# Splitting the gathered rows of a segment sum into two float32r parts on the chip

## The chip, the cores and the metric
The kernel runs on one core of one Trainium2 chip. The metric is the time of one execution on the device in microseconds (us). Below, PE is TensorE's matmul stream, PEld its weight loads, DVE is VectorE, ACT is ScalarE, POOL is GpSimd and SP is SyncE.

## The reference
Two graph layers over 3125 nodes with 256 features and 100,000 edges. The second layer, in which the change lies, is cut here to what matters:

```
proj = jnp.einsum('ni,rio->rno', feat, Wb)          # 16 relations, 3125 nodes, 256 features
m    = proj[etypes, dst] + backward_bias            # one gathered row of 256 floats per edge
m    = m / degree(src)[src]
m_backward = segment_sum(m, src, num_segments=3125)  # summed into the node that the edge leaves
out = x + 2*(feat @ loop_weight) + self_bias + m_forward + m_backward
```

## The kernel before
The work is in stages, one after the other. Layer one goes over the edges in 196 supertiles of 512 (512 = 4 groups of 128, `J = 4`). Then PE projects all nodes for each of the relations, the forward rows are gathered and summed while PE makes the backward projections, and last come the backward rows. VectorE has sorted the edges by source on the way.

The last stage, called the backward stage below, is the one that the change touches. It runs over 196 supertiles (`ST`) with four engines:

- GpSimd gathers the rows (`gather_rows`, L429): four indirect DMAs for a supertile, each of 128 rows of 1 KB, with the row numbers read from `row_dst` in SBUF. They go into a ring of buffers `raw2` with `RS = 12` places in SBUF (inside the tile `hr`). Before the first of four it waits until PE has read the place for the last time (`s_agg[2]`). All of this is unrolled code, so GpSimd has nothing between the gathers but that wait.
- VectorE compares the source numbers of the 512 edges with the 256 nodes of a window of two blocks (`compare2`, recorded at L1013) and so writes a one-hot matrix of 128 x 1024 floats into a ring of six (`HS = 6`, in the tile `fa`). One of its inputs, `iota_p`, lies in PSUM.
- PE multiplies (`products2`, L731): for each half of the window four matmuls of 128x258 in float32, 8 in all, into one of three pairs of PSUM banks. Columns 256 and 257 of a row are ones, so that the sum counts the edges too.
- VectorE adds the pair of sums to `acc` (`add2`, L1070). Where the sources of a supertile reach beyond the two blocks, a further one-hot, four further matmuls and a further addition follow (L1013, L731 with `pc`, L1078).

VectorE's code is a loop over six supertiles, PE's one over twelve. At the top of each pass VectorE loads the packed windows of ten supertiles from SBUF into registers (`windows_of`, L281), which takes no engine time but holds back what follows. The order of VectorE's work is written out by hand in `backward`: for supertile s it first compares for s + 4, then adds the sums of s.

Ahead of the backward stage lies a short passage in which VectorE and ScalarE finish the forward means and clear `acc` (L1296, L1349, L592, L595). The gathers of the backward stage already run in it. After the stage `backward_mean` scales the sums (L1291) and SP stores the output.

float32r is the type of the operands of PE's single-pass matmuls in this kernel. Layer one already works so: ScalarE casts a tile to float32r (the high part, L520), VectorE subtracts that from the tile (the low part, L1026), and PE multiplies both parts.

Of the kernel before, what the change touches and what calls it, by code (L numbers as in the profile page):

```python
# [41 lines left out]
QS = 24  # L42
RS = 12
HS = 6
# [4 lines left out]
assert ST % GS == 0 and COLS % RG == 0 and ST % RG == 0 and SI == S1 * (NQ // 2) + 2 == 2 * (S2 + QS)  # L49
assert (ST - GS) % RS == 0 and (ST - GS) % (2 * RF) == 0 and 2 * QS % RF == 0  # L50


def gnn_program(nc, x, dst_l, src_l, typ_l, ea_t, W1, b1, W2, b2, Wg, bg, gamma, beta,
# [9 lines left out]
    with ctx:  # L63
# [6 lines left out]
        def sem(name):  # L70
            return ctx.enter_context(nc.semaphore(name))
# [80 lines left out]
        slot_iota, slot_base = srt[:, 0:P].bitcast(I32), srt[:, P:P + NB].bitcast(I32)  # L152
        raw2 = hr[:, 0:RS * J * AW].bitcast(F32).rearrange("p (a j f) -> p a j f", a=RS, j=J)
        onehot2 = [fa[:, c:c + 2 * SE].rearrange("p (j n) -> p j n", j=J) for c in (8192, 9216, 4224, 5248, 2064, 3096)]
        further_onehot = fa[:, 6272:6272 + SE].rearrange("p (j n) -> p j n", j=J)
        PARTS = ((1, 0), (0, 1), (0, 0))
# [69 lines left out]
        s_xadd = [sem(f"s_xadd{k}") for k in range(3)]  # L226
        s_ones = sem("s_ones")
        s_xagg = [sem(f"s_xagg{k}") for k in range(3)]
        s_self = sem("s_self")
# [147 lines left out]
        def _(pool):  # L377
# [67 lines left out]
            for s in range(ST):  # L445
                if s >= RS:
                    pool.wait_ge(s_agg[2], s - RS + 2)
                gather_rows(raw2[:, s % RS, :, :], proj[1][:, :], row_dst, s, s_gath[2][s % RS])


        @block.scalar
        def _(act):
# [135 lines left out]
            for b in range(NB + 2):  # L588
# [4 lines left out]
                if b >= 2:  # L593
                    act.wait_ge(s_scaled, b - 1)
                    nc.scalar.copy(acc[:, b - 2, :], iota[:, 0:1].to_broadcast([P, AW])).then_inc(s_zero[1], 1)  # L595

        @block.tensor
        def _(pe):
# [126 lines left out]
            def sum_backward(s, n, rnd, w):  # L725

                lo, hi, wx = w

                def products2(out, keys):
                    for j in range(J):  # L730
                        last = nc.tensor.matmul(out[:, 0:AW], keys[:, j, :], raw2[:, n, j, :], start=(j == 0), stop=(j == J - 1))  # L731
                    return last

                pe.wait_ge(s_oh[2], s + 1)
                pe.wait_ge(s_gath[2][n], 16 * J * (rnd + 1))
                if past(s, 3):
                    pe.wait_ge(s_add[2], s - 2)
                for c in range(2):
                    last = products2(pair_sums[n % 3][:, c, :], onehot2[n % HS][:, :, c * P:(c + 1) * P])
                last.then_inc(s_agg[2], 1)  # L740
                with pe.If(hi > lo + 1):
                    with pe.Fori(lo + 2, hi + 1) as b:
                        pe.wait_ge(s_xadd[2], wx + b)
                        pe.wait_ge(s_xoh[2], wx + b)
                        products2(further_sums, further_onehot).then_inc(s_xagg[2], 1)
# [94 lines left out]
        def _(dve):  # L840
# [509 lines left out]
            dve.wait_ge(s_mean, NB)  # L1350
            nc.vector.memset(raw2[:, :, :, H:AW], 1.0).then_inc(s_ones, 1)
            dve.wait_ge(s_zero[1], NB)

            def backward(s0, n0, w, ahead):
                for m in range(len(w)):
                    if m + 4 < len(w):
                        compare2(s0 + m + 4, (n0 + m + 4) % HS, w[m + 4])
# [3 lines left out]
            for n, w2 in enumerate(windows_of(dve, 1, 2, 2)):  # L1361
                compare2(n + 2, n + 2, w2)
            backward(0, 0, windows_of(dve, 1, 0, 2 * GS), GS)
            with dve.Fori(0, (ST - GS) // HS - 1) as i:
# [49 lines left out]
```

## Time and profile before

| what | value |
|---|---|
| time, median of 3 runs | 3745.22 us (3745.19 to 3745.71) |
| time of the profiled execution | 3743.66 us |
| its span in the profile | 3741.9 us |
| busy PE, DVE, ACT, POOL | 86%, 66%, 27%, 67% of the span |
| DMA | 569.99 MB, mean 152 GB/s |
| granted TensorE clock, mean | 0.975 of full speed |

The span is that of one profiled execution; its own time is 1.8 us longer than the span, and the median of the other runs is 1.6 us above that time. Busy shares are means over stages with different limits; the backward stage begins at about 2737 us, when GpSimd starts its gathers, and ends at about 3725 us.

### The profile page before, as it was taken

The page shows a single profiled execution, that of the slowest core. Times are in us where ns is not written, and L with a number is a line of the kernel's source. Part 1 is how long each engine was busy: PE and PEld are TensorE (multiplying, and loading weights), DVE is VectorE, ACT ScalarE, POOL GpSimd, SP SyncE. Part 2 cuts the span into 40 slices and gives each one's busy share as a digit, 9 for nine tenths or more (in the row PEclk, how much of TensorE's full clock was granted, in tenths as well). Part 3 has the DMA queues.
Part 4 walks back from the last instruction along what each step waited for, and adds up shares of the span by engine and source line. Part 5 has one row for each costly group of instructions (what it writes and reads, how often), then busy time and mean ns, then how long its engine had stood idle before and what let it go on. Part 6 is the DMA issues. An engine that isn't in the chain of part 4 may idle for free.

```text
span 3741.9 us, 72813 instructions
## 1 busy us (share of the span) xinstructions
PE 3212.6 (86%) x21136; PEld 2761.7 (74%) x21137; DVE 2457.5 (66%) x3369; ACT 1001.5 (27%) x1563; POOL 2492.5 (67%) x3139
## 2 busy tenths in 40 slices
PE   5999999999999996999877788878867778777775
PEld 4999999999999995787665566656656666665654
DVE  6899999999999998887666663223254344444433
ACT  3555555555555554443111111111120000000000
POOL 1777777777777770001777777777777777777775
PEclk8999999999999998999999999999989999999999
DMA  4666666666566652665555557555543333333333
GB/s 165 178 176 177 173 176 172 176 168 177 171 174 171 171 171 74 201 207 187 165 166 164 162 167 175 166 156 165 165 116 105 105 105 105 105 105 105 105 105 114
DMA packets 322755, 569.99 MB, mean 152 GB/s; under 512 B 73896, under 2 KB 218392, under 8 KB 322584
## 3 DMA queue, kind: packets, MB, share of 16 engines
q0 software_dynamic: 137984, 411.19, 39.1%
q1 hardware_dynamic: 182732, 154.33, 13.0%
q10 hardware_dynamic: 1868, 2.52, 0.2%
q8 instruction: 67, 1.10, 0.1%
q14 instruction: 104, 0.85, 0.1%
HBM read 452.43 MB, written 115.41 MB: 152 GB/s over the span
## 4 chain that ended last, share of the span: by engine, by line
PE 45%; POOL 25%; issue 13%; DVE 11%; DMA 1%; DVEq 1%; ACT 1%; POOLq 0%; ACTq 0%
POOL hr L429 16%; PE pc L679 14%; PE pa L689 10%; PE pu L669 5%; PE pg L653 4%; DVE tops L1229 4%; POOL fa L429 4%; DVE key L1232 4%; PE pu L661 3%; POOL ws L429 2%; PE pu L731 1%; POOL rows_b L429 1%; PE pu L786 1%; PE pc L641 1%; PE pa L731 1%
## 5 line engine op out<-in xcount | busy, mean ns | idle before, releaser
L410 POOL DMA_INDIRECT fa<-ptab,slot x784 | 774.9, 988 | 323.9 <-issue 254.6
L429 POOL DMA_INDIRECT hr<-proj,row_dst x784 | 741.6, 946 | 238.7 <-issue 237.2
L429 POOL DMA_INDIRECT fa<-proj,row_src x400 | 378.8, 947 | 466.3 <-DMA proj<-fa 343.5
L679 PE MATMUL pc<-ws,hr 128*128 128x256 f32 x4704 | 603.4, 284 | 0.0
L679 PEld LDWEIGHTS pc<-ws,hr 128*128 128x128 f32 x4704 | 570.3, 189 | 0.5 <-issue 0.5
L689 PE MATMUL pa<-fa,onehot 128*128 128x256 f32 x904 | 241.3, 417 | 125.3 <-issue 57.4
L731 PE MATMUL pu<-hr,fa 128*128 128x258 f32 x1056 | 248.0, 387 | 78.6 <-issue 43.0
L689 PEld LDWEIGHTS pa<-fa,onehot 128*128 128x128 f32 x904 | 178.9, 205 | 183.8 <-issue 157.4
L1013 DVE SCALAR_TENSOR_TENSOR fa<-pc,base,src_f 128x1024 f32<-128x1024 f32 (+1 forms) x210 | 261.8, 1248 | 74.8 <-issue 63.6
L1046 DVE TENSOR_TENSOR acc<-acc,pa 128x256 f32 x196 | 82.1, 419 | 342.6 <-PE pa L689 341.2
L731 PE MATMUL pg<-hr,fa 128*128 128x258 f32 x1040 | 241.5, 384 | 63.7 <-issue 49.3
L520 ACT CAST hr<-fa 128x1024 fp32r<-128x1024 f32 x196 | 205.9, 1051 | 331.1 <-DVE fa L1020 331.1
L731 PE MATMUL pa<-hr,fa 128*128 128x258 f32 x1040 | 241.2, 384 | 61.2 <-issue 50.4
L731 PEld LDWEIGHTS pu<-hr,fa 128*128 128x128 f32 x1056 | 197.8, 191 | 126.7 <-issue 56.7
L509 ACT ACTIVATE hr<-pu 128x512 fp32r<-128x512 f32 x392 | 213.2, 597 | 252.9 <-PE pu L669 252.9
L1020 DVE TENSOR_TENSOR fa<-fa,pc 128x1024 f32<-128x1024 f32 x196 | 239.3, 1221 | 60.5 <-PE pc L679 59.3
L731 PEld LDWEIGHTS pg<-hr,fa 128*128 128x128 f32 x1040 | 192.9, 189 | 110.1 <-issue 64.8
L731 PEld LDWEIGHTS pa<-hr,fa 128*128 128x128 f32 x1040 | 193.0, 189 | 106.9 <-issue 66.1
L1026 DVE TENSOR_TENSOR hr<-fa,hr 128x1024 fp32r<-128x1024 f32 x196 | 241.2, 1231 | 24.1 <-ACT hr L520 8.7
L689 PE MATMUL pa<-hr 128*128 128x258 f32 (+1 forms) x1760 | 248.2, 284 | 5.7 <-issue 3.6
L786 PE MATMUL pu<-hr 128*128 128x512 f32 x960 | 246.0, 399 | 1.4 <-DVE hr L1172 0.7
L997 DVE SCALAR_TENSOR_TENSOR hr<-pu,hr 128x1024 fp32r<-128x1024 f32 x196 | 238.1, 1215 | 3.6 <-ACT hr L509 3.5
(167 smaller groups left out, 5653.2 us busy)
## 6 DMA issues: line engine op xcount, KB each, us to landing
proj<-fa SPq DMA_DIRECT2D x400, 256.0 KB, 2.4
fa<-in_ea_t SPq DMA_DIRECT2D x196, 128.0 KB
fa<-ptab,slot POOLq DMA_INDIRECT x784
hr<-proj,row_dst POOLq DMA_INDIRECT x784, 2.7
fa<-in_Wrel SPq DMA_DIRECT2D x32, 256.0 KB, 3.7
ptab<-fa SPq DMA_DIRECT2D x25, 256.0 KB, 2.0
fa<-proj,row_src POOLq DMA_INDIRECT x400, 3.0
ws<-proj,row_src POOLq DMA_INDIRECT x192
```

The lines of the kernel that those rows point to most:

```text
L410: pool.indirect_dma_start(pbuf[:, n % 2, j, :], None, ptab[:, :], bass.IndirectOffsetOnAxis(ap=slot[:, n, j:j + 1], axis=0)).then_inc(s_ga ...
L429: pool.indirect_dma_start(buffer[:, j, 0:H], None, table, bass.IndirectOffsetOnAxis(ap=rows[:, J * s + j:J * s + j + 1], axis=0)).then_inc ...
L509: last = nc.scalar.activation(uT[:, par, 0, h, :, :].rearrange("p k e -> p (k e)"), pu[:, h, :], ACT.Relu)
L520: nc.scalar.copy(msg[:, par, 0, :, :], gate[:, par, :, :]).then_inc(s_mhi, 1)
L679: last = nc.tensor.matmul(pc[:, j, :], uT[:, par, a, j // 2, kk, j % 2 * P:(j % 2 + 1) * P], w2s[:, c, kk, :], start=False, stop=(j == jj ...
L689: last = nc.tensor.matmul(pa[:, bank, 0:width], keys[:, at, j, :], rows[:, j, :], start=(n == 0), stop=(n == len(todo) - 1))
L731: last = nc.tensor.matmul(out[:, 0:AW], keys[:, j, :], raw2[:, n, j, :], start=(j == 0), stop=(j == J - 1))
L786: last = nc.tensor.matmul(pslots[n], hT[:, a, kk, b * P:(b + 1) * P], wsp[:, u, c, kk, :], start=(not d and m == 0 and kk == 0), stop=(m = ...
L997: nc.vector.scalar_tensor_tensor(out=uT[:, par, 1, :, :, :].rearrange("p h k e -> p h (k e)"), in0=pu[:, :, :], scalar=0.0, in1=uT[:, par, ...
L1013: return nc.vector.scalar_tensor_tensor(out=out, in0=numbers.unsqueeze(1).to_broadcast([P, J, width]), scalar=base[:, bass.ds(b, 1)], in1= ...
L1020: nc.vector.tensor_tensor(gate[:, par, :, :], gate[:, par, :, :], pc[:, :, :], ALU.mult).then_inc(s_msg, 1)
L1026: nc.vector.tensor_tensor(msg[:, par, 1, :, :], gate[:, par, :, :], msg[:, par, 0, :, :], ALU.subtract).then_inc(s_mlo, 1)
```

## The change
- Each gathered supertile is split on the chip. ScalarE casts it to float32r into `high2` (`rows_high`), VectorE subtracts that from the raw rows into `low2` (`rows_low`), both rings of three places (`RP2 = 3`) in float32r. The ones of the count stand in `high2` alone.
- `products2` makes 16 float32r matmuls for a supertile instead of 8 in float32: for each half of the window four of 128x258 with the high part and four of 128x256 with the low part.
- The ring of raw rows has six places instead of twelve (three in `hr`, three in `fa`), and GpSimd takes a place again once `rows_low` has read it (`s_rowlo`), no longer after PE. PE waits for `s_rowlo` instead of the gathers' semaphores.
- The one-hots become float32r and move from `fa` to `hr`. PE's loop covers six supertiles instead of twelve.
- In `backward`, VectorE does `rows_low` of supertile s + 1 first, then `compare2` of s + 4, then `add2` of s.

```diff
-RS = 12
+RS = 6
+RP2 = 3
...
-        raw2 = hr[:, 0:RS * J * AW].bitcast(F32).rearrange("p (a j f) -> p a j f", a=RS, j=J)
-        onehot2 = [fa[:, c:c + 2 * SE].rearrange("p (j n) -> p j n", j=J) for c in (8192, 9216, 4224, 5248, 2064, 3096)]
...
+        raw2 = [t.rearrange("p (j f) -> p j f", j=J) for t in
+                [hr[:, c:c + J * H].bitcast(F32) for c in (12824, 13848, 14872)] + [fa[:, c:c + J * H] for c in (4224, 5248, 8192)]]
+        high2 = hr[:, 0:RP2 * J * AW].rearrange("p (a j f) -> p a j f", a=RP2, j=J)
+        low2 = hr[:, 3096:3096 + RP2 * J * H].rearrange("p (a j f) -> p a j f", a=RP2, j=J)
+        onehot2 = [hr[:, c:c + 2 * SE].rearrange("p (j n) -> p j n", j=J) for c in range(6168, 6168 + 2 * SE * HS, 2 * SE)]
...
                 if s >= RS:
-                    pool.wait_ge(s_agg[2], s - RS + 2)
-                gather_rows(raw2[:, s % RS, :, :], proj[1][:, :], row_dst, s, s_gath[2][s % RS])
+                    pool.wait_ge(s_rowlo, s - RS + 1)
+                gather_rows(raw2[s % RS], proj[1][:, :], row_dst, s, s_gath[2][s % RS])
...
+            def rows_high(s, n, rnd):
+
+                act.wait_ge(s_gath[2][n], 16 * J * (rnd + 1))
+                if past(s, RP2):
+                    act.wait_ge(s_agg[2], s - RP2 + 2)
+                nc.scalar.copy(high2[:, n % RP2, :, 0:H], raw2[n]).then_inc(s_rowhi, 1)
...
                 def products2(out, keys):
-                    for j in range(J):
-                        last = nc.tensor.matmul(out[:, 0:AW], keys[:, j, :], raw2[:, n, j, :], start=(j == 0), stop=(j == J - 1))
+                    todo = [(j, part) for part in (high2, low2) for j in range(J)]
+                    for t, (j, part) in enumerate(todo):
+                        rows = part[:, n % RP2, j, :]
+                        last = nc.tensor.matmul(out[:, 0:rows.shape[1]], keys[:, j, :], rows, start=(t == 0), stop=(t == len(todo) - 1))
                     return last
 
                 pe.wait_ge(s_oh[2], s + 1)
-                pe.wait_ge(s_gath[2][n], 16 * J * (rnd + 1))
+                pe.wait_ge(s_rowlo, s + 1)
...
-            nc.vector.memset(raw2[:, :, :, H:AW], 1.0).then_inc(s_ones, 1)
+            nc.vector.memset(high2[:, :, :, H:AW].bitcast(F32), 1.0).then_inc(s_ones, 1)
             dve.wait_ge(s_zero[1], NB)
+
+            def rows_low(s, n):
+
+                dve.wait_ge(s_rowhi, s + 1)
+                nc.vector.tensor_tensor(low2[:, n % RP2, :, :], raw2[n], high2[:, n % RP2, :, 0:H],
+                                        ALU.subtract).then_inc(s_rowlo, 1)
 
             def backward(s0, n0, w, ahead):
                 for m in range(len(w)):
+                    if m < len(w) - max(ahead, 1):
+                        rows_low(s0 + m + 1, (n0 + m + 1) % RS)
                     if m + 4 < len(w):
                         compare2(s0 + m + 4, (n0 + m + 4) % HS, w[m + 4])
...
             for n, w2 in enumerate(windows_of(dve, 1, 2, 2)):
                 compare2(n + 2, n + 2, w2)
+            rows_low(0, 0)
```

How VectorE's instructions stand at the top of its loop over six supertiles, before. The first row is the load of the windows into registers, L1013 the comparison, L1070 the addition; the names of semaphores end in 2 for the backward stage.

```order
L281 TENSOR_LOAD win
L1058 REGISTER_ALU
L1013 REGISTER_ALU [waits s_agg2]
L1013 ISA
L1013 SCALAR_TENSOR_TENSOR fa<-pc,base,src_f 128x1024
L1065 REGISTER_ALU x3
L1065 ISA
L1068 REGISTER_ALU [waits s_add2,s_xadd2]
L1070 ISA [waits s_agg2]
L1070 TENSOR_TENSOR acc<-acc,pg 128x516
```

The same place after the change (line numbers of the changed kernel: L287 the load, L1378 the subtraction of `rows_low`, L1034 the comparison, L1091 the addition).

```order
L287 TENSOR_LOAD win
L1377 REGISTER_ALU
L1378 TENSOR_TENSOR hr<-fa,hr 128x1024 [waits s_rowhi]
L1079 REGISTER_ALU
L1034 REGISTER_ALU [waits s_agg2]
L1034 ISA
L1034 SCALAR_TENSOR_TENSOR hr<-pc,base,src_f 128x1024
L1086 REGISTER_ALU x3
L1086 ISA
L1089 REGISTER_ALU [waits s_add2,s_xadd2]
L1091 ISA [waits s_agg2]
L1091 TENSOR_TENSOR acc<-acc,pg 128x516
```

One subtraction with both inputs in SBUF now stands ahead of the comparison in every supertile, and at the top of the loop it stands behind the load.

ScalarE had no instruction in this stage before. Its loop after the change is this (L608 the cast; the waits on `s_gath2_n` are for the four gathers of a supertile):

```order
L607 REGISTER_ALU [waits s_gath2_0]
L608 CAST hr<-hr 128x4x256 [waits s_agg2]
L607 REGISTER_ALU [waits s_gath2_1]
L608 CAST hr<-hr 128x4x256 [waits s_agg2]
L607 REGISTER_ALU [waits s_gath2_2]
L608 CAST hr<-hr 128x4x256 [waits s_agg2]
```

The wait for the gathers stands on a register instruction ahead of the cast, as it does in layer one before at the top of ScalarE's loop (L519 ahead of the cast L520):

```order
L519 REGISTER_ALU [waits s_msg]
L520 CAST hr<-fa 128x4x256 [waits s_add0]
```

## Rows read from the trace of the kernel before

**Rows 1.** Windows view: busy us and (count) of each engine, granted clock, DMA share, GB/s.

```profile
3200.00:3400.00 200.00, 156.44 (x681) 126.09 (x681) 84.25 (x91) 0.00 (x0) 151.27 (x161) 1.00 0.36 105
```

**Rows 2.** Source view of L429, 2737 to 3742 us: ns min/median/max, first and last start.

```profile
L429 POOL DMA_INDIRECT hr<-proj,row_dst x784: 942/946/1248, 2737.7 to 3716.9; - x196
...
  issue: 237.2, 779
...
DMA to landing us min/median/max: 2.6/2.7/4.2
```

**Rows 3.** Waits view, 2800 to 3700 us: us in total, times, longest us.

```profile
DVE acc L1070 <- PE pu L731: 162.5, 61, 3.2
...
DVE fa L1013 <- issue: 61.3, 28, 2.9
```

**Rows 4.** Timeline of the end: start us, us, engine, line, idle before and its releaser.

```profile
3716.94 0.95 POOL L429 DMA_INDIRECT hr<-proj,row_dst  x1 [0.30 <-issue]
...
3719.72 3.35 PEld L731 LDWEIGHTS pu<-hr,fa 128*128 128x128 f32 x16 [1.59 <-issue]
3719.75 3.73 PE L731 MATMUL pu<-hr,fa 128*128 128x258 f32 x16 [1.22 <-issue]
3723.72 0.69 DVE L1070 TENSOR_TENSOR acc<-acc,pu 128x516 f32 x1 [4.25 <-PE pu L731]
```

**Rows 5.** Timeline of the forward gathers, where VectorE splits weights (L1172).

```profile
2152.98 1.23 DVE L1172 TENSOR_TENSOR hr<-fa,hr 128x1024 fp32r<-128x1024 f32 x1
2153.23 1.80 POOL L429 DMA_INDIRECT ws<-proj,row_src  x1 [0.30 <-issue]
...
2522.20 0.95 POOL L429 DMA_INDIRECT fa<-proj,row_src  x1 [0.30 <-issue]
2522.76 1.22 DVE L1172 TENSOR_TENSOR hr<-fa,hr 128x1024 fp32r<-128x1024 f32 x1
2523.45 1.35 POOL L429 DMA_INDIRECT fa<-proj,row_src  x1 [0.30 <-issue]
```

**Rows 6.** Timeline of layer one: a gather and a subtraction that start nearly together.

```profile
1358.42 0.97 POOL L410 DMA_INDIRECT fa<-ptab,slot  x1 [0.15 <-issue]
1358.47 1.23 DVE L1026 TENSOR_TENSOR hr<-fa,hr 128x1024 fp32r<-128x1024 f32 x1
```

**Rows 7.** Timeline of layer one: cast, subtraction and eight float32r matmuls.

```profile
1053.20 1.11 PE L689 MATMUL pa<-hr 128*128 128x258 f32 x8
1054.66 1.05 ACT L520 CAST hr<-fa 128x1024 fp32r<-128x1024 f32 x1 [1.27 <-DVE fa L1020]
1055.74 1.25 DVE L1026 TENSOR_TENSOR hr<-fa,hr 128x1024 fp32r<-128x1024 f32 x1
...
1204.08 1.22 DVE L1020 TENSOR_TENSOR fa<-fa,pc 128x1024 f32<-128x1024 f32 x1
1205.41 1.05 ACT L520 CAST hr<-fa 128x1024 fp32r<-128x1024 f32 x1 [1.33 <-DVE fa L1020]
```

**Rows 8.** Timeline where the backward stage gets under way.

```profile
2763.20 6.50 PE L731 MATMUL pu<-hr,fa 128*128 128x258 f32 x16 [19.39 <-DVE hr L1351]
2763.70 3.67 DVE L1013 SCALAR_TENSOR_TENSOR fa<-pc,base,src_f 128x1024 f32<-128x1024 f32 x3 [0.55 <-issue]
...
2768.05 0.96 POOL L429 DMA_INDIRECT hr<-proj,row_dst  x1 [0.30 <-issue]
```

**Rows 9.** Source view of L1078, and timeline of one further block and one loop top.

```profile
L1078 DVE TENSOR_TENSOR acc<-acc,pc x14: 423/424/426, 2952.4 to 3487.5; 128x258 f32 x14
...
3097.29 1.28 DVE L1013 SCALAR_TENSOR_TENSOR fa<-pc,base,src_f 128x1024 f32<-128x1024 f32 x1 [2.90 <-issue]
...
3108.60 0.69 DVE L1070 TENSOR_TENSOR acc<-acc,pu 128x516 f32 x1 [3.06 <-PE pu L731]
3109.30 0.75 DVE L1013 SCALAR_TENSOR_TENSOR fa<-pc,base,src_f 128x512 f32<-128x512 f32 x1
3110.20 1.98 PE L731 MATMUL pc<-hr,fa 128*128 128x258 f32 x8 [1.75 <-DVE fa L1013]
3112.39 0.43 DVE L1078 TENSOR_TENSOR acc<-acc,pc 128x258 f32 x1 [2.34 <-PE pc L731]
```

More of the change, by code:

```diff
@@ L49 @@
 assert ST % GS == 0 and COLS % RG == 0 and ST % RG == 0 and SI == S1 * (NQ // 2) + 2 == 2 * (S2 + QS)
-assert (ST - GS) % RS == 0 and (ST - GS) % (2 * RF) == 0 and 2 * QS % RF == 0
+assert HS == RS and RS % RP2 == 0 and (ST - GS) % RS == 0 and (ST - GS) % (2 * RF) == 0 and 2 * QS % RF == 0
 def gnn_program(nc, x, dst_l, src_l, typ_l, ea_t, W1, b1, W2, b2, Wg, bg, gamma, beta,
@@ L152, in gnn_program @@
         slot_iota, slot_base = srt[:, 0:P].bitcast(I32), srt[:, P:P + NB].bitcast(I32)
-        raw2 = hr[:, 0:RS * J * AW].bitcast(F32).rearrange("p (a j f) -> p a j f", a=RS, j=J)
-        onehot2 = [fa[:, c:c + 2 * SE].rearrange("p (j n) -> p j n", j=J) for c in (8192, 9216, 4224, 5248, 2064, 3096)]
-        further_onehot = fa[:, 6272:6272 + SE].rearrange("p (j n) -> p j n", j=J)
+        raw2 = [t.rearrange("p (j f) -> p j f", j=J) for t in
[3 more added lines that the diff above has]
+        onehot2 = [hr[:, c:c + 2 * SE].rearrange("p (j n) -> p j n", j=J) for c in range(6168, 6168 + 2 * SE * HS, 2 * SE)]
+        further_onehot = hr[:, 12312:12312 + SE].rearrange("p (j n) -> p j n", j=J)
         PARTS = ((1, 0), (0, 1), (0, 0))
@@ L227, in gnn_program @@
         s_ones = sem("s_ones")
+        s_rowhi = sem("s_rowhi")
+        s_rowlo = sem("s_rowlo")
         s_xagg = [sem(f"s_xagg{k}") for k in range(3)]
@@ L595, in _ @@
                     nc.scalar.copy(acc[:, b - 2, :], iota[:, 0:1].to_broadcast([P, AW])).then_inc(s_zero[1], 1)
+            def rows_high(s, n, rnd):
[3 more added lines that the diff above has]
+                nc.scalar.copy(high2[:, n % RP2, :, 0:H], raw2[n]).then_inc(s_rowhi, 1)
+            for n in range(GS):
+                rows_high(n, n, 0)
+            with act.Fori(0, (ST - GS) // RS) as i:
+                for m in range(RS):
+                    rows_high(RS * i + GS + m, (GS + m) % RS, i + (GS + m) // RS)
         @block.tensor
```

## The prediction
> **What bounds the kernel now.** The windows view of the backward stage comes first [rows 1]. In 200 us PE is busy for 156.4, VectorE for 84.3 and GpSimd for 151.3, so no engine is full and the shares alone don't decide. The source view of the gathers decides [rows 2]. 784 gathers start between 2737.7 and 3716.9 us, one each (3716.9 - 2737.7) / 783 = 1.2506 us, of which 0.946 are the instruction and 0.30 its issue; 779 of 784 idle times ahead of them end by nothing but issue. GpSimd never waits for PE's hand-back. It makes a supertile of four gathers in 5.00 us, and the other two engines live inside that: VectorE waits for PE for up to 3.2 us at the additions [rows 3], and PE's 16 records of a supertile take 3.73 us and begin 2.78 us after the supertile's last gather has started, that is on its landing [rows 4]. So the stage lasts 196 x 5.00 us whatever PE does below 5.00, and faster matmuls are worth something only behind the last gather.
>
> **The change part by part.**
>
> *PE.* Eight float32r matmuls of 258 and 256 columns take 1.11 us at full clock [rows 7], 16 some 2.1 us against 3.73. Inside the stage this is worth nothing, since the gathers cover it; were that cover gone, it would be 196 x 1.6 = 314 us. At half the clock, which PE has after it stood idle for 19 us (the first supertile takes 6.50 instead of 3.73 us [rows 8]), 16 would take 4.2 us, which is still below 5.00.
>
> *The end.* The last gather starts at 3716.94 and PE's load at 3719.72 [rows 4]. ScalarE can begin its cast a little later than PE its load: where the wait stands on a register instruction, as in the new loop, the cast L520 starts 0.11 us after its releaser (1204.08 + 1.22 to 1205.41), elsewhere 0.04 [rows 7]. That is 2.78 + 0.07 = 2.85 us after the gather's start. Cast 1.05, 0.03 to VectorE (1054.66 + 1.05 to 1055.74), subtraction 1.22 [rows 5, 7]: the low part is there at 5.15, and PE ends 0.06 + 2.1 later, at 7.3 us behind the gather instead of 6.54. The end costs +0.8 us, with half the clock +2.9. I take +1.
>
> *Rings.* A place is handed back about 3.75 + 5.15 = 8.9 us after the supertile's first gather, and is wanted again after 6 x 5.00 = 30. Only the start is close: supertile 6 wants its place at 2768.05 [rows 8]. VectorE is through with the two comparisons that stand ahead of `rows_low(0)` at about 2766.2 (two of the three in 3.67 us), so the first place is free at 2767.4. No stall, with 0.6 us to spare.
>
> *What the subtraction does to the gathers.* This is the term that decides. `rows_low` has both inputs in SBUF. The forward stage has such a subtraction too, L1172, and gathers beside it [rows 5]. L1172 runs from 2152.98 to 2154.21; a gather that starts at 2153.23 takes 1.80 us instead of 0.95: 0.85 more, and 2154.21 - 2153.23 - 0.85 = 0.13. L1172 runs from 2522.76 to 2523.98; the gather at 2523.45 takes 1.35, 0.40 more, and again 0.53 - 0.40 = 0.13. The gather at 2522.20, under way when L1172 began, took 0.95. So a gather that starts while such a subtraction runs needs something 0.13 us after its start which it gets only when the subtraction ends, and all later gathers move by the same time. A gather that starts ahead of the subtraction is safe, even by 0.05 us: it takes its usual 0.97 [rows 6].
>
> The Trainium skill ("SBUF — State Buffer", Who interferes with whom) says that a VectorE instruction with two SBUF inputs contends with a GpSimd instruction that reads SBUF, and that whichever came first holds the port for its whole length; the trace agrees, as the rows show. The same section also says that a probe saw `tensor_tensor` not stall DMA and infers that making descriptors needs another port; by that sentence the stage would keep its 1.25 us a gather and the sum would be +1 us. The measured rows decide against it here, and it stays as a rival.
>
> Now the phase. Count from the start of a supertile's last gather. The next gathers start at 1.25, 2.50, 3.75, 5.00. The subtraction begins at 2.85 + 1.05 + 0.03 = 3.93 and ends at 5.15. A gather is held if it starts behind the subtraction and its start + 0.13 lies before the subtraction's end. The one at 3.75 started first, by 0.18; the one at 5.00 wants its port at 5.13, 0.02 before the end. So the usual supertile costs 0.02 us, and with the spread of the landings (2.6 at least, 2.7 in the median [rows 2]) about 0.03: 166 x 0.03 = 5 us. It matters that the phase renews itself: landing, cast and subtraction all follow the last gather, so a shift of the gathers shifts them too.
>
> *Loop tops.* VectorE's cycle is subtraction 1.22, comparison 1.28, addition 0.69. Where they follow directly each starts some 0.08 before the last has ended (three comparisons in 3.67 us [rows 8]), so the cycle is 3.0 us and the next subtraction is due only after 5.00. At the top of its loop the load of the windows stands in between. The idle time from an addition to the next comparison there is 2.90 us at the long ones [rows 9]; 28 such times sum to 61.3 [rows 3], so some are short (about 1.5) and about 16 of 32 long. `rows_low` has two register instructions less ahead of it than the comparison, for which I take off 0.2: 3.0 + 2.7 = 5.7, late by 0.7. It then ends at 5.85 and the gather at 5.00 is held for 5.85 - 5.13 = 0.7. 16 x 0.7 = 11 us. The short ones come in time.
>
> *Further blocks.* 14 supertiles have one [rows 9]. Addition's start to that of the further one is 3.79 us (3108.60 to 3112.39), of which 1.98 are matmuls that now take 1.11: 2.9, plus 0.43. VectorE is free at 2.35 + 2.9 + 0.43 = 5.7 after its subtraction began, late by 0.65, and the gather at 5.00 is held for about 0.65. 14 x 0.65 = 9 us.
>
> *Start.* Until VectorE has caught up with the gathers, some six to eight subtractions fall without a fixed phase: 0.5 us each, 4 us.
>
> The sum: 5 + 11 + 9 + 4 + 1 = +30 us. Against the profiled execution's own time, 3743.7 + 30 = 3773.7; the median of the runs shown is 1.6 us above it, so 3775.
>
> **The rivals.**
> 1. *The phase lies later.* If the landing, the cast or its wait takes 0.1 to 0.3 us more, each usual supertile costs that on top: 166 x 0.1 = 17 us to 166 x 0.3 = 50 us, 3790 to 3825. For it: the margin is 0.02 us and nothing of the order gather, ScalarE, VectorE has been seen together.
> 2. *The phase slips ahead.* If the subtraction starts 0.2 us or more earlier, at 3.71 say, the gather at 3.75 is held for 3.71 + 1.22 - 3.88 = 1.05 us in nearly every supertile: up to 196 x 1.05 = +205 us, at half of them about +100. 3850 to 3950. Against it: 0.2 us is more than the spread of most landings.
> 3. *The gathers are not held* (the end on the other side): the held gathers of the forward stage have another cause, and what is left is the end, +1 us, 3746; with PE's clock at half in the end +3, 3748. It decides if in the usual supertiles and at the loop tops the gathers stay at 0.946 us. For it: the 784 gathers of this stage ran at 946 ns while VectorE worked 42% of the time; against it, those operations have an input in PSUM and are another kind.
> 4. *The stage is PE's after all* and the float32r products shorten it: each 0.1 us a supertile would give 20 us. Against it stand 779 idle times that end by issue. Little is left for it.
>
> **How the numbers follow.** Forecast (+15 to +45 us): 0.60. Rival 1: 0.15. Rival 2: 0.09. Rival 3: 0.10, nearly all within 0.2% (7.5 us, what a measurement of this kernel can tell from no change). Between 3752.7 and 3760: 0.04. Rival 4: 0.02. The range 3756 to 3828 takes in the forecast, rival 1 and part of what lies between. Faster 0.02, same 0.11, slower 0.87.
>
> **What the changed profile would show.** The gathers: a median near 0.95 to 1.00 us, a mean near 0.98 (30 us over 784), some 40 of them over 1.25, and the last one starting near 3746. Those long ones begin inside a subtraction and end its end + 0.82. PE's busy share near 42% in the stage. ScalarE with 196 casts of 1.05 us. VectorE's subtraction begins 3.9 us behind the last gather. I would be wrong if the held gathers show up in every supertile (rival 2), if there are none (rival 3), or if GpSimd's idle time names the wait for `rows_low` for more than a microsecond, which would mean that the ring of six binds.

## The result and the profile after

The changed kernel takes 3766.08 us, the median of 5 runs (3760.5 to 3767.08), and the kernel before, run beside it, 3745.22 (5 runs, 3743.63 to 3748.19). The ratio is 1.005, 95% interval 1.0038 to 1.0061: slower, by about 21 us.

The windows view of the changed kernel over the same stretch as [rows 1], in the same columns:

```profile
3200.00:3400.00 200.00, 118.78 (x669) 111.00 (x669) 124.83 (x129) 41.29 (x40) 151.87 (x158) 0.79 0.36 103
```

PE's busy time fell from 156.4 to 118.8 us, VectorE's rose from 84.3 to 124.8, ScalarE came in with 40 casts, and GpSimd, which sets the pace, has done 158 gathers where it had done 161.

The source view of the gathers (L435 now), 2737 to 3770 us, to be read against [rows 2]. `raw2` now lies partly in `fa`, so there are two groups, with min/median/max in ns and the first and last start:

```profile
L435 POOL DMA_INDIRECT hr<-proj,row_dst x396: 942/946/1889, 2741.3 to 3731.9; - x198
L435 POOL DMA_INDIRECT fa<-proj,row_dst x388: 942/946/1965, 2756.7 to 3736.9; - x194
...
  issue: 239.6, 787
```

The median is as before, but the longest took 1.97 us instead of 1.25, and still no idle time of GpSimd ends by a wait for another engine. The groups view of the same stretch has the sums (busy us, mean ns of one, idle us and its releaser):

```profile
L435 POOL DMA_INDIRECT hr<-proj,row_dst x396 | 385.8, 974 | 120.5 <-issue 120.5
L435 POOL DMA_INDIRECT fa<-proj,row_dst x388 | 372.1, 959 | 118.2 <-issue 118.2
```

385.8 + 372.1 = 757.9 us, where 784 x 0.946 = 741.7 were to be had: 16.2 us more. From first to last start it is 3736.86 - 2741.34 = 995.5 us instead of 979.2 [rows 2], 16.3 more. All of the stage's loss is in the durations of its gathers.

The spans differ by 3764.4 - 3741.9 = 22.5 us, and they divide so:

| part | us |
|---|---|
| ahead of the first gather (2737.7 to 2741.3) | 3.6 |
| first to last gather | 16.3 |
| last gather's start to the end (24.9 to 27.5) | 2.6 |

The first part can't be shown to be the change's: in the nine profiled executions of this study the first backward gather starts anywhere between 2737.2 and 2741.3, and both ends are kernels that contain the change (e4 and the changed kernel).

What one held gather looks like, in the timeline of the changed kernel at the start of the stage (start us, us, engine, line, idle before and its releaser):

```profile
2787.16 0.94 POOL L435 DMA_INDIRECT hr<-proj,row_dst  x1 [0.30 <-issue]
2787.75 1.22 DVE L1378 TENSOR_TENSOR hr<-hr 128x1024 fp32r<-128x1024 f32 x1
2788.41 1.38 POOL L435 DMA_INDIRECT hr<-proj,row_dst  x1 [0.30 <-issue]
```

The gather under way when the subtraction begins is untouched. The next starts inside it and ends at 2789.79, which is the subtraction's end, 2788.97, and 0.82: the same sum as for L1172 [rows 5].

And a usual supertile, one whose subtraction is 0.05 us later than the median, in the timeline of the same kernel near the end of the stage:

```profile
3724.30 0.95 POOL L435 DMA_INDIRECT hr<-proj,row_dst  x1 [0.30 <-issue]
3724.69 1.05 ACT L608 CAST hr<-hr 128x1024 fp32r<-128x1024 f32 x1 [4.06 <-DMA hr<-proj,row_dst]
...
3725.55 0.94 POOL L435 DMA_INDIRECT hr<-proj,row_dst  x1 [0.30 <-issue]
3725.77 1.22 DVE L1378 TENSOR_TENSOR hr<-hr 128x1024 fp32r<-128x1024 f32 x1 [2.08 <-ACT hr L608]
...
3726.80 1.01 POOL L435 DMA_INDIRECT hr<-proj,row_dst  x1 [0.30 <-issue]
```

The subtraction begins 0.22 us behind one gather and ends at 3726.99; the next gather starts at 3726.80 and wants its port at 3726.93, so it is held for 0.06. In the trace the subtraction begins 3.92 us after the start of the supertile's last gather in the median of the 156 usual ones (three in four by 3.96, nine in ten by 3.99) and ends at 5.15; 3.93 and 5.15 were predicted.

There is one exception to the rule that a gather behind the subtraction's start is held:

```profile
2970.17 1.29 DVE L1378 TENSOR_TENSOR hr<-hr 128x1024 fp32r<-128x1024 f32 x1 [0.26 <-ACT hr L608]
2970.20 0.95 POOL L435 DMA_INDIRECT hr<-proj,row_dst  x1 [0.30 <-issue]
```

The gather starts 0.034 us behind and takes its usual time, and it is the subtraction that takes 1.29 us instead of 1.22. In the changed kernel, e3, e4 and e5 this happens to nine gathers, all of which start within 0.043 us. From 0.048 us on every one is held: in the changed kernel, e2, e3 and e5 that is 601 gathers, and the rule gives the hold of each to within 0.02 us.

### The profile page after: what moved, and what is told of

It reads as the page before. It is cut to its first block, busy times and chain, and to the rows that moved or that the text cites. A ratio compares the mean times of both kernels' runs of the same rounds, so it can differ in the third digit from the quotient of the medians.

```text
span 3764.4 us, 73607 instructions
## 1 busy us (share of the span) xinstructions
PE 3058.4 (81%) x21136; PEld 2713.5 (72%) x21137; DVE 2664.0 (71%) x3565; ACT 1207.0 (32%) x1759; POOL 2511.6 (67%) x3139
## 4 chain that ended last, share of the span: by engine, by line
PE 40%; POOL 31%; issue 13%; DVE 10%; DMA 1%; DVEq 1%; ACT 1%; POOLq 0%; ACTq 0%
POOL fa L435 15%; PE pc L698 14%; POOL hr L435 10%; PE pa L708 9%; PE pu L688 5%; PE pg L672 4%; DVE tops L1250 4%; DVE key L1253 4%; PE pu L680 3%; POOL ws L435 3%; POOL rows_b L435 1%; POOL rows_a L435 1%; PE pc L660 1%; PE pu L807 1%; PE pg L807 1%
## 5 line engine op out<-in xcount | busy, mean ns | idle before, releaser
L435 POOL DMA_INDIRECT fa<-proj,row_src x400 | 380.6, 952 | 467.2 <-DMA proj<-fa 344.1
L435 POOL DMA_INDIRECT hr<-proj,row_dst x396 | 385.8, 974 | 120.5 <-issue 120.5
L435 POOL DMA_INDIRECT fa<-proj,row_dst x388 | 372.1, 959 | 118.2 <-issue 118.2
L752 PE MATMUL pg<-hr 128*128 128x258 f32 (+1 forms) x1040 | 191.0, 355 | 122.0 <-issue 62.6
L752 PE MATMUL pu<-hr 128*128 128x258 f32 (+1 forms) x1056 | 183.7, 342 | 125.8 <-issue 102.1
L752 PE MATMUL pa<-hr 128*128 128x258 f32 (+1 forms) x1040 | 189.7, 353 | 111.5 <-issue 57.5
L752 PEld LDWEIGHTS pg<-hr 128*128 128x128 f32 x1040 | 177.3, 258 | 134.4 <-issue 134.4
L752 PEld LDWEIGHTS pu<-hr 128*128 128x128 f32 x1056 | 171.3, 246 | 138.2 <-issue 138.1
L752 PEld LDWEIGHTS pa<-hr 128*128 128x128 f32 x1040 | 176.6, 257 | 124.8 <-issue 124.8
L1034 DVE SCALAR_TENSOR_TENSOR hr<-pc,base,src_f 128x1024 fp32r<-128x1024 f32 (+1 forms) x210 | 260.9, 1243 | 1.4 <-DVE win L920 0.8
L708 PE MATMUL pa<-hr 128*128 128x258 f32 (+1 forms) x1760 | 248.9, 284 | 5.3 <-issue 3.2
```

Source lines behind the costliest of these rows:

```text
L435: pool.indirect_dma_start(buffer[:, j, 0:H], None, table, bass.IndirectOffsetOnAxis(ap=rows[:, J * s + j:J * s + j + 1], axis=0)).then_inc ...
L708: last = nc.tensor.matmul(pa[:, bank, 0:width], keys[:, at, j, :], rows[:, j, :], start=(n == 0), stop=(n == len(todo) - 1))
L752: last = nc.tensor.matmul(out[:, 0:rows.shape[1]], keys[:, j, :], rows, start=(t == 0), stop=(t == len(todo) - 1))
L1034: return nc.vector.scalar_tensor_tensor(out=out, in0=numbers.unsqueeze(1).to_broadcast([P, J, width]), scalar=base[:, bass.ds(b, 1)], in1= ...
```

## The experiments

The phase of a subtraction is the time from the start of its supertile's last gather to its own start. Theory A is the prediction's: a subtraction with both inputs in SBUF holds a gather that starts behind it, until the subtraction ends. The rivals are that the loss comes from VectorE's or ScalarE's added work as such, from the smaller ring, from PE's slower clock, or that the hold belongs to some other property of the subtraction. A hold is the time that a gather takes over its usual 0.946 us.

**e1_one_input**: all of the change stays, with its order, waits and bytes, but the subtraction's first input is in PSUM. The subtraction itself is left out: `low2` receives the raw rows. The operation is of another kind too, `scalar_tensor_tensor`; e7 keeps the kind.

```diff
-                nc.vector.tensor_tensor(low2[:, n % RP2, :, :], raw2[n], high2[:, n % RP2, :, 0:H],
-                                        ALU.subtract).then_inc(s_rowlo, 1)
+                nc.vector.scalar_tensor_tensor(out=low2[:, n % RP2, :, :], in0=fbias_p.unsqueeze(1).to_broadcast([P, J, H]), scalar=0.0,
+                                               in1=raw2[n], op0=ALU.mult, op1=ALU.add).then_inc(s_rowlo, 1)
```

> The changed kernel, with rows_low as a VectorE operation of the same size that has one input in SBUF and one in PSUM (0 times the bias in PSUM plus the raw rows). It leaves out the subtraction: the low part is the whole row. Theory A (the subtraction with two SBUF inputs holds the gathers): no gather of the backward stage over 1.1 us, the sum of what the gathers take over 0.946 us falls from 16 us to under 1, the last one starts 980 us after the first as in the kernel before, and the time is 16 us under the changed kernel's: 3750 us, 2 to 7 us over the kernel before (the end, and whatever lies ahead of the stage). Theory B (some other part of the split, such as the six places, ScalarE's reads or more work on VectorE, slows the gathers): long gathers stay, 3766 us.

Measured: 3746.21 us (11 runs), ratio to the kernel before 1.0002 (0.9993 to 1.0011). Timeline of this kernel behind a further block, where VectorE is late and its instructions lie anywhere:

```profile
3087.91 1.23 DVE L1378 SCALAR_TENSOR_TENSOR hr<-pc,hr 128x1024 fp32r<-128x1024 f32 x1 [0.19 <-ACT hr L608]
3087.98 0.95 POOL L435 DMA_INDIRECT fa<-proj,row_dst  x1 [0.30 <-issue]
```

The gather starts 0.07 us behind an instruction of 1.23 us, the worst place there is, and takes 0.95. The longest gather is the second, with 1.25 us, as it is in the kernel before (1248 ns in [rows 2]), and no other is over 0.97, though 118 gathers begin inside such an instruction; their durations over 0.946 sum to -0.1 us, and first to last start is 979.2 us as before. So this edit is worth 995.5 - 979.2 = 16.3 us of the gathers. The medians differ by 3766.1 - 3746.2 = 19.9 us; 2.5 of that is the start of the stage (2738.9 instead of 2741.3 in the traces). The rest of the change costs the gathers nothing. Its end is there, 27.5 us from the last gather's start instead of 24.9, but 2.6 us can't be told from the spread of the runs here (3743.9 to 3748.2), and the median came 0.7 us over the kernel before where 2 to 7 were expected.

**e2_before_plus_sub**: the other direction. The kernel before gets only the suspect, a subtraction with both inputs in SBUF whose result nobody reads, and a ring of six handed back by the additions to make room. It waits for the gathers directly, so it comes earlier in the phase.

```diff
-RS = 12
+RS = 6
...
-                    pool.wait_ge(s_agg[2], s - RS + 2)
+                    pool.wait_ge(s_add[2], s - RS + 2)
...
+            def read_rows(s, n, rnd):
+
+                dve.wait_ge(s_gath[2][n], 16 * J * (rnd + 1))
+                at = 12800 + n % 3 * J * H
+                nc.vector.tensor_tensor(hr[:, at:at + J * H].rearrange("p (j f) -> p j f", j=J), raw2[:, n, :, 0:H], raw2[:, n, :, 0:H],
+                                        ALU.subtract)
...
+                    if m < len(w) - max(ahead, 1):
+                        read_rows(s0 + m + 1, (n0 + m + 1) % RS, r0 + (n0 + m + 1) // RS)
...
```

> The kernel before with six raw places and an added VectorE subtraction of a gathered supertile from itself into unused SBUF, as soon as the gathers have landed; PE still multiplies the raw rows in float32. Theory A with the phase rule (a gather that starts behind the subtraction's start wants its port 0.13 us after its own start and waits to the subtraction's end): it starts 2.8 us behind the last gather, ends at 4.03, and the gather at 3.75 is held to 4.03 - 3.88 = 0.15 us in every supertile: 196 x 0.15 = 29 us, with 5 to 9 us for further blocks and the start and 5 for the six places, 3745 + 42 = 3787 us, most gathers third of their supertile at about 1.10 us. If holds are there but fall at random: 0.5 us each, 3745 + 100. Theory B: 3750 us, what six places cost alone.

Measured: 3787.81 us (4 runs), ratio 1.0114 (1.0099 to 1.013). One supertile in its timeline:

```profile
3300.23 1.23 DVE L1358 TENSOR_TENSOR hr<-hr 128x1024 fp32r<-128x1024 f32 x1 [2.08 <-DMA hr<-proj,row_dst]
...
3301.23 1.04 POOL L429 DMA_INDIRECT hr<-proj,row_dst  x1 [0.30 <-issue]
```

The gather at 3301.23 is held by 3301.46 - 3301.23 - 0.13 = 0.10 us, as measured. The holds sum to 38.2 us, 25.5 of them at the third gather of a supertile; the rest of the 42 us is one wait of GpSimd for the smaller ring, some 5 us (e6). The suspect alone brings a loss of the same kind, and a supertile pays what its phase says.

**e3_later_cast**: the changed kernel with the cast in four pieces, which makes nothing but its end later.

```diff
-                nc.scalar.copy(high2[:, n % RP2, :, 0:H], raw2[n]).then_inc(s_rowhi, 1)
+                for j in range(J):
+                    last = nc.scalar.copy(high2[:, n % RP2, j, 0:H], raw2[n][:, j, :])
+                last.then_inc(s_rowhi, 1)
```

> The changed kernel with ScalarE's cast in four pieces of 128x256, so that the subtraction begins later; the same values. Four casts of 0.40 us that overlap a little take 1.3 to 1.6 us instead of 1.05: the subtraction begins 4.2 to 4.4 us behind the last gather instead of 3.92. Theory A with the phase rule: each usual supertile costs the shift, 0.25 to 0.5 us at the fourth gather: 166 x 0.25 to 0.5 = +42 to +83 us over the changed kernel, 3808 to 3849 us. If the phase doesn't matter: +1 us at the end, 3767 us.

Measured: 3804.84 us (4 runs), ratio 1.0161 (1.0146 to 1.0177). Its timeline:

```profile
3299.18 1.32 ACT L609 CAST hr<-fa 128x256 fp32r<-128x256 f32 x4 [3.97 <-DMA fa<-proj,row_dst]
...
3300.54 1.22 DVE L1380 TENSOR_TENSOR hr<-fa,hr 128x1024 fp32r<-128x1024 f32 x1 [2.27 <-ACT hr L609]
3301.35 1.23 POOL L435 DMA_INDIRECT fa<-proj,row_dst  x1 [0.30 <-issue]
```

The four casts take 1.32 us instead of 1.05, so the subtraction comes 0.27 later, and the gather that starts 5.00 us behind the supertile's last one is held by 0.27 us in the median of all supertiles: 47.6 us there and 54.8 in all. That is 0.27 us of ScalarE's time turned into 39 us of the whole. The time is 3 us under the expected 3808 to 3849. It is rival 1 of the prediction, brought about on purpose, near its price (166 x 0.27 = 45 us).

**e4_split_halves**: cast and subtraction in two halves each, so that the low part is ready earlier.

```diff
-                nc.scalar.copy(high2[:, n % RP2, :, 0:H], raw2[n]).then_inc(s_rowhi, 1)
+                for h in (0, 2):
+                    nc.scalar.copy(high2[:, n % RP2, h:h + 2, 0:H], raw2[n][:, h:h + 2, :]).then_inc(s_rowhi, 1)
...
-                dve.wait_ge(s_rowhi, s + 1)
-                nc.vector.tensor_tensor(low2[:, n % RP2, :, :], raw2[n], high2[:, n % RP2, :, 0:H],
-                                        ALU.subtract).then_inc(s_rowlo, 1)
+                for h in (0, 2):
+                    dve.wait_ge(s_rowhi, 2 * s + 1 + h // 2)
+                    last = nc.vector.tensor_tensor(low2[:, n % RP2, h:h + 2, :], raw2[n][:, h:h + 2, :], high2[:, n % RP2, h:h + 2, 0:H],
+                                                   ALU.subtract)
+                last.then_inc(s_rowlo, 1)
```

> The changed kernel with cast and subtraction each in two halves of 128x512, so that the first subtraction begins before the gather at 3.75 us behind the last one; the same values. The first half of the cast takes 0.6 us from 2.83, the first subtraction runs from about 3.45 to 4.13. Phase rule: the gather at 3.75 starts behind it, wants its port at 3.88 and is held to 4.13, 0.25 us in each usual supertile: 160 x 0.25 = +40 us over what the changed kernel has in its usual supertiles (2 us), some 3803 us, nearly all at the third gather of a supertile. If the second subtraction, which follows at about 4.1, takes the port before the waiting gather gets it, the hold goes to 4.75 or so: 0.85 us each, +135 us, 3900. If only the length of a subtraction mattered, shorter ones would hold less: 3766 us or less.

Measured: 3805.09 us (4 runs), ratio 1.0161 (1.0145 to 1.0177). Its timeline, the two halves in one row:

```profile
3301.90 1.29 DVE L1380 TENSOR_TENSOR hr<-fa,hr 128x512 fp32r<-128x512 f32 x2 [2.26 <-ACT hr L609]
3302.12 1.29 POOL L435 DMA_INDIRECT fa<-proj,row_dst  x1 [0.30 <-issue]
```

The supertile's last gather started at 3298.37 (two gathers ahead of the one shown, 3299.62 and 3300.88, belong to the next), so the low part is there 4.82 us behind it instead of 5.14. The price is a hold at the third gather of nearly every supertile (164 of 196), 49.1 us there and 58.6 in all, since the subtraction now begins ahead of that gather. The gather shown lost 1.29 - 0.95 = 0.34 us, which ends its hold at 3302.12 + 0.13 + 0.34 = 3302.59, in the middle of the pair and not at its end. So a waiting gather gets through between two subtractions that follow one another directly, and a pair costs no more than its first half.

**e5_pe_float32**: is PE's speed worth anything now? The changed kernel with PE's eight float32 products as before, on the high part and the one-hots. The low product is left out.

```diff
-                    todo = [(j, part) for part in (high2, low2) for j in range(J)]
-                    for t, (j, part) in enumerate(todo):
-                        rows = part[:, n % RP2, j, :]
-                        last = nc.tensor.matmul(out[:, 0:rows.shape[1]], keys[:, j, :], rows, start=(t == 0), stop=(t == len(todo) - 1))
+                    for j in range(J):
+                        last = nc.tensor.matmul(out[:, 0:AW], keys[:, j, :].bitcast(F32), high2[:, n % RP2, j, :].bitcast(F32),
+                                                start=(j == 0), stop=(j == J - 1))
```

> The changed kernel with PE's products as before: 8 float32 matmuls of 128x258 on the high part alone, in place of 16 in float32r. It leaves out the product with the low part, while cast and subtraction go on. If PE's speed is worth nothing in the stage: the same 16 us of holds but for 2 or 3 us at the 14 further blocks, PE's busy share back at 75% or more with the clock at full speed, the end the same as in the changed kernel (one step of 3.7 us behind the low part, there because of half the clock, here of float32): 3766 us, within 4. If the single passes were worth what PE's busy time lost: 1.3 us a supertile and more, over 3850 us.

Measured: 3777.57 us (5 runs), ratio 1.0092 (1.0078 to 1.0105). The expectation of 3766, within 4, missed by 11. The waits view of this kernel, 2741 to 3740 us (us in total, times, longest):

```profile
ACT hr L608 <- PE pa L750: 63.5, 15, 7.4
ACT hr L608 <- PE pg L750: 51.5, 11, 11.7
ACT hr L608 <- PE pu L750: 40.1, 9, 6.3
```

In 35 supertiles the cast waits until PE has left a place of `high2`, a ring of three. In the changed kernel the same rows of that view say:

```profile
ACT hr L608 <- PE pg L752: 25.5, 5, 8.8
...
ACT hr L608 <- PE pa L752: 18.4, 6, 4.3
ACT hr L608 <- PE pu L752: 15.9, 4, 5.2
```

that is 15 supertiles. Each such wait puts a subtraction off its phase, and the holds sum to 30.2 us instead of 16.3; past the start, all but two of the holds over 0.1 us (those two are 0.13 and 0.10) lie in the supertiles behind a further block. PE's speed has no worth of its own in this stage, as predicted, but once the holds exist it shortens the catch-up in which they fall.

**e6_before_ring6**: the kernel before with the ring of six alone, still handed back by PE.

```diff
-RS = 12
+RS = 6
```

> The kernel before with a ring of six raw places instead of twelve, handed back by PE as before. It tells what the six places cost alone. PE's first supertile ends at 2769.7 us and its second at 2773.2; supertile 6 wants its place at 2768.05 and gets it only then: one wait of 5 us at the start, none afterwards since PE then keeps ahead. 3745 + 5 = 3750 us. If the six places bind in the steady stage too: well over 3755 us.

Measured: 3750.53 us (11 runs), ratio 1.0013 (1.0004 to 1.0022). The waits view of GpSimd, 2737 to 2900 us, has one wait:

```profile
POOL hr L429 <- PE pg L731: 5.9, 1, 5.9
```

It is the first reuse of a place, while PE is behind at the start. In the changed kernel VectorE hands the place back ahead of PE, and GpSimd waits nowhere. The prediction's "no stall, with 0.6 us to spare" held (the first subtraction ends at 2770.94 and the gather that wants its place starts at 2772.06), and that part of the change saves what its own smaller ring would cost.

**e7_raw_in_psum**: a version with the changed kernel's values and without the holds. ScalarE copies the raw rows into PSUM as well (into `pa`, so that two pairs of banks are left for the sums), and the subtraction reads them there. PE's wait for the additions and the index of the sums (`n % 2`) follow from two pairs.

```diff
-        pair_sums = [pu[:, :, :], pg[:, :, :].rearrange("p (a j) f -> p a (j f)", a=2), pa[:, :, :]]
+        pair_sums = [pu[:, :, :], pg[:, :, :].rearrange("p (a j) f -> p a (j f)", a=2)]
+        raw_p = pa[:, :, :].rearrange("p a e -> p (a e)").rearrange("p (j f) -> p j f", j=J)
...
-                nc.scalar.copy(high2[:, n % RP2, :, 0:H], raw2[n]).then_inc(s_rowhi, 1)
+                nc.scalar.copy(high2[:, n % RP2, :, 0:H], raw2[n])
+                if past(s, 1):
+                    act.wait_ge(s_rowlo, s)
+                nc.scalar.copy(raw_p, raw2[n]).then_inc(s_rowhi, 1)
...
-                nc.vector.tensor_tensor(low2[:, n % RP2, :, :], raw2[n], high2[:, n % RP2, :, 0:H],
+                nc.vector.tensor_tensor(low2[:, n % RP2, :, :], raw_p, high2[:, n % RP2, :, 0:H],
```

> The changed kernel with the same values, but ScalarE, behind the cast, also copies the raw rows into two PSUM banks, and the subtraction reads them there: one input in SBUF, one in PSUM. The sums take turns in two pairs of banks instead of three. Theory A: the subtraction no longer holds a gather, all of the 16 us goes; ScalarE's second operation puts 1.0 us more on the end: 3766 - 16 + 1 = 3751 us by the changed kernel's time, 3748 by the kernel before's plus 2.5 for the end and 1. Theory B, that the split itself costs it: 3766 us or more, since ScalarE now has twice the work. Two pairs instead of three would show as PE waiting for the addition; I expect none, since the addition of s - 1 ends ahead of the subtraction of s + 1.

Measured: 3749.08 us (11 runs), ratio 1.001 (1.0001 to 1.0019). Its timeline:

```profile
3304.97 1.23 DVE L1382 TENSOR_TENSOR hr<-pa,hr 128x1024 fp32r<-128x1024 f32 x1 [1.92 <-ACT pa L612]
3305.27 0.95 POOL L436 DMA_INDIRECT fa<-proj,row_dst  x1 [0.30 <-issue]
```

Here it is the same `tensor_tensor`, 1.23 us long, with a gather that starts 0.30 us behind it and takes 0.95. In all, 185 gathers of this run begin inside a subtraction, and the longest of them takes 0.96. First to last start is 979.7 us, with one wait of GpSimd for a place of the ring at the start (0.8 us over its usual 0.30). With e1 this excludes the rival of another property: the same operation, the same output, one input moved, and no hold. It is 17 us faster than the changed kernel for the same values, and still some 4 us slower than the kernel before; the end, with one more copy in its chain, is 28.4 us instead of 24.9.

## Why the prediction was right

The forecast was +30 us, 3775, with 3756 to 3828 as the range; measured were +21. The mechanism held: the holds of the gathers, as read from two gathers of the forward stage, are the loss (e1, e2, e7), and their size follows from the phase to within 0.02 us (0.10 in e2, 0.27 in e3, each from the one rule "the subtraction's end less the gather's start less 0.13").

The rule of the Trainium skill ("SBUF — State Buffer", Who interferes with whom) that a VectorE instruction with two SBUF inputs contends with a GpSimd instruction that reads SBUF agrees with all of these runs. The runs show the hold itself; that a port is what both want is the skill's account. The prediction also called it borne out by the trace that whichever came first holds the port for its whole length. The rows bear that out for the subtraction alone. A gather that came first doesn't hold back the subtraction: in the changed kernel subtractions begin 0.08 to 0.2 us into a gather of 0.95, as at 3725.77 above, 0.03 us after their cast has ended, and take 1.22 us all the same. The only trace of it is the 0.07 us of the exception above. And e4's held gather got through between two halves. The same section's sentence that a `tensor_tensor` doesn't stall DMA, by which the result would have been about 3746, is contradicted for these indirect gathers by 16.3 us of holds in the changed kernel, which are gone in e1 and e7.

By the terms of the sum:

| term | predicted | measured |
|---|---|---|
| usual supertiles | 5 | 2.4 |
| loop tops | 11 | 0 by themselves |
| behind further blocks | 9 | 8.3, of which up to 2.3 with a load |
| start | 4 | 5.6 |
| the end | 1 | 2.6 |

The measured holds are added up from the gathers' durations over 0.946: the first 13 supertiles are the start; after them 22 holds over 0.06 us lie within 11 us behind a further block's addition, 8.3 us; the rest, with nine holds of 0.06 to 0.16 us, is the usual supertiles'.

*Loop tops* is the term that failed, and it failed by its step "the cycle is 3.0 us ... 3.0 + 2.7 = 5.7, late by 0.7". It put the load of the windows behind the addition's start, where it stood before. But before, the addition itself waited for PE (162.5 us in 61 waits [rows 3]), and so held back the load queued behind it (there the load at 3304.7 starts 0.94 us behind the addition's start, and nearly all of the 31 between 2800 and 3700 us start 0.94 to 0.98 behind it). In the changed kernel the addition finds its sums ready, and the queue runs ahead. The waits view, 2800 to 3700 us, has eight such waits of this kind in all, 3.7 us; its largest row is

```profile
DVE acc L1091 <- PE pu L752: 1.4, 3, 0.5
```

Source view of L287, one pass of the loop (ns, start; DVEq is VectorE's queue):

```profile
L287 DVEq TENSOR_LOAD <-win x1: 2297/2297/2297, 3536.7 to 3536.7; - x1
```

and the timeline of VectorE there:

```profile
3534.91 1.22 DVE L1378 TENSOR_TENSOR hr<-fa,hr 128x1024 fp32r<-128x1024 f32 x1 [2.01 <-ACT hr L608]
...
3537.25 0.68 DVE L1091 TENSOR_TENSOR acc<-acc,pu 128x516 f32 x1
3539.97 1.23 DVE L1378 TENSOR_TENSOR hr<-fa,hr 128x1024 fp32r<-128x1024 f32 x1 [2.04 <-ACT hr L608]
```

The load starts 1.8 us after the subtraction does, ahead of the addition, and is through at 3539.0; the next subtraction begins at 3539.97, on ScalarE's release. Of the 30 loads between 2800 and 3700 us, 24 are through ahead of the next subtraction, the long ones by 0.93 to 1.07 us. All over the stage the source view of the subtraction says the same (ns, then idle us ahead of it, times):

```profile
L1378 DVE TENSOR_TENSOR hr<-hr x99: 1217/1225/1292, 2769.7 to 3735.8; 128x1024 fp32r<-128x1024 f32 x99
...
  ACT hr L608: 325.7, 166
  issue: 10.0, 5
```

The other six loads fall where VectorE is behind, and there the step of the prediction does hold: the subtraction starts 0.12 us after the load's end. One lies in the start, five behind further blocks. The first holds behind those five sum to 2.3 us (0.92, 0.60, 0.56, 0.13, 0.07) and stand in the table with the further blocks. Whether they would have fallen without the load isn't shown.

*Further blocks* came close to the predicted 9 us by another path. Timeline of one:

```profile
3082.12 1.23 DVE L1378 TENSOR_TENSOR hr<-fa,hr 128x1024 fp32r<-128x1024 f32 x1 [1.96 <-ACT hr L608]
...
3085.94 2.05 PE L752 MATMUL pc<-hr 128*128 128x258 f32 x8 [5.15 <-DVE hr L1034]
...
3088.21 0.42 DVE L1099 TENSOR_TENSOR acc<-acc,pc 128x258 f32 x1 [2.41 <-PE pc L752]
3088.23 0.94 POOL L435 DMA_INDIRECT hr<-proj,row_dst  x1 [0.30 <-issue]
3088.55 1.22 DVE L1378 TENSOR_TENSOR hr<-hr 128x1024 fp32r<-128x1024 f32 x1
3089.48 1.11 POOL L435 DMA_INDIRECT hr<-proj,row_dst  x1 [0.30 <-issue]
```

The eight matmuls take 2.05 us and not 1.11, since PE is at half its clock in such a moment (granted 0.50 from 3085.9 to 3088.0). So the subtraction is late by 1.4 us and not 0.65, and the gather of 3088.23, on which the hold was to fall, has started first and is safe. The next one is held by 0.16. In the supertiles behind, VectorE catches up on 5.00 us with a cycle of about 3, its subtractions pass over several gathers, and some lose up to 1.0 us. The sum agreed by luck, the step didn't: one hold of 0.65 for each block was expected, and the runs show one to three of 0.07 to 1.02 us behind 13 of the 14 blocks. Four of the five idle times by issue above, 8.5 of the 10.0 us, lie in the same catch-ups.

*Usual supertiles*: 0.015 us each and not 0.03. The subtraction begins 0.01 us earlier than it was put, and the margin that this term rests on is 0.02. *Start*: 5.6 for 4, eleven holds. *The end* was given as +1, with +2.9 for half the clock, and the latter came. Timeline of the end of the changed kernel, against [rows 4]:

```profile
3736.86 0.96 POOL L435 DMA_INDIRECT fa<-proj,row_dst  x1 [0.30 <-issue]
3739.76 1.05 ACT L608 CAST hr<-fa 128x1024 fp32r<-128x1024 f32 x1 [4.02 <-DMA fa<-proj,row_dst]
3740.84 1.23 DVE L1378 TENSOR_TENSOR hr<-fa,hr 128x1024 fp32r<-128x1024 f32 x1 [3.23 <-ACT hr L608]
...
3742.16 3.76 PE L752 MATMUL pu<-hr 128*128 128x258 f32 x16 [1.30 <-issue]
...
3746.17 0.69 DVE L1091 TENSOR_TENSOR acc<-acc,pu 128x516 f32 x1 [3.51 <-PE pu L752]
```

Cast and subtraction lie within 0.05 us of where they were put (2.90 and 3.98 us behind the gather); the matmuls take 3.76 us instead of 2.1. In e4 the last sixteen ran at full clock and took 2.14 us, and its end was 25.4 us.

Of the marks that the prediction named, the gathers' median (0.946) and their lack of waits came true; the mean is 0.967 and not 0.98, 21 gathers and not 40 take 1.25 or more, as the loop tops are missing. PE is busy 59% and not 42%: the 42 were for full clock.

*The rivals.* The phase lying later (1) did not occur but is real, as e3 shows. The phase slipping ahead (2) did not occur; in e2 and e4, where the subtraction comes earlier, the holds are at the third gather, which is that case at another offset. Gathers not held (3) is refuted by the changed kernel's holds, and another cause of them by e1 and e7. PE as the bound (4) is refuted by the result, in which PE's busy time fell and the stage grew, and by e5: with PE busy 78% instead of 59% in 200 us no gather waits.

Left open: part of the difference between the medians (20.9) and the holds with the end (18.9) is the start of the stage, which lies up to 4 us apart in the nine profiled executions. And no run tried to make a gather itself cheaper, which the 1.25 us that bound every version here ask for.

## What to carry to other kernels

Where a stream of indirect gathers is the bound, ask of each VectorE instruction beside it whether both its inputs lie in SBUF; if they do, lay its start and end over the gathers' starts, since a shift of 0.27 us decided over 39 us. One input in PSUM removed the holds altogether (e7), even though it took a copy on another engine; what stayed, some 4 us, lies outside them. And before pricing a delay at a loop's top, ask which wait held the load back before, and whether the change removes that wait.

## What the runs showed of the hardware

- A held gather gets through between two VectorE instructions that follow one another directly: 0.34 us held and not about 0.9 (e4).
- A gather that starts up to 0.043 us behind a `tensor_tensor` with two SBUF inputs isn't held, and the `tensor_tensor` takes 1.26 to 1.30 us instead of 1.22 (changed kernel, e3, e5); one that starts 0.048 us or more behind is held to its end.
- The load of ten supertiles' windows into VectorE's registers took about 1.07 and about 2.30 us in turn, in both kernels; the 30 loads of the changed kernel between 2800 and 3700 us range from 1064 to 2332 ns. Why was not looked into.
- PE's granted clock went between its two levels, 1.2 and 2.4 GHz, all through the changed stage: its mean is 0.79 over the 200 us shown first, in which PE's sixteen matmuls of a supertile are followed by idle time, and 1.00 before [rows 1]. So PE's busy time fell to 118.8 us and not to the 84 that sixteen matmuls at full clock in every 5.00 us would make.
